# A graph layer's mix block: its second half moved into the edge batches

## The chip, the cores and the metric

The kernel runs on one NeuronCore of a Trainium2 chip. The metric is device time in microseconds (us) for one execution of the whole program. The program is one launch; every intermediate lies in on-chip memory or in scratch tensors in device memory.

## The reference, cut to what matters

A layer over 3125 nodes with 256 features each and 50000 edges sorted by target. `xn` is the layer norm of `x`. Three things are computed from it:

```python
xn  = layernorm(x)
# 1. graph attention: keys, queries, values by node type (6), edges of 3 types,
#    softmax over all the edges of a type, 8 heads
agg = segment_sum(w[..., None] * V[src] @ Wm[t], dst)
gnn = layernorm(agg + xn) * ln_g + ln_b
# 2. mix block (linear attention, 8 heads, then an MLP), here with its two halves
t   = linear_attention(elu(xn Wq) + 1, elu(xn Wk) + 1, xn Wv)
x1  = layernorm(t + xn) * ln1_g + ln1_b                     # first half
h   = gelu(x1 @ W1.T + b1)                                   # second half
mix = layernorm(h @ W2.T + b2 + x1) * ln2_g + ln2_b          # second half
x   = x + gnn + mix
# 3. a gated feed-forward part on layernorm(x): the top half of the rows by a score
x   = x + ffn(layernorm(x))
```

All sums are in float32. An output row needs the sum of its edges' messages, its mix row and its feed-forward row.

## The kernel before, in words

The nodes lie in NT = 25 tiles of 128 rows. The node tables (key and value rows, query rows) are made by node type in NS = 30 tiles, into which the rows are sorted. The edges lie in NB = 49 batches of two groups (NG = 98); a group gathers its key and value rows by four indirect DMAs of 256 KB on GpSimd's queue (POOL), into one of RING slots.

Every engine has its own instruction stream, written out by hand in the order in which it runs, and the streams meet at semaphores. There are four stages:

*Front*: layer norm of x, tables of the edges, the state of the linear attention.

*Tables and mix* (about 80 to 290 us): 30 steps, one per table tile. Step s works on table tile s and on mix tiles at several ages. TensorE (PE) runs in a step: mix_q, keys_values (L921), mix_t (L972) of the tile before, mix_turn (L996) of the one before that, queries (L932), mix_h (L985) of m-3, turn_in (L896) of the next table tile, by_type (L909), and mix_y (L1006, L1007) of m-4. turn_in turns the next tile's rows in bank ps[0], which queries uses too, so it waits until VectorE (DVE) has taken the queries out (g_qc). ScalarE (ACT) has in its step centre, the elu with an Exp (L776), affine (L784), a weights' copy, the gelu of m-3 (L794), turn_in's copy (L727) and q_out (L745). DVE has residual (L1299 to L1302), kv_out, elu, q_bias_in, attend, finish (L1308 to L1314) and shift. POOL has two pairs of reciprocal square roots (L657, L658), the product `gained` (L667), the load of the table rows two tiles ahead (L631) and the stores of the tables (L642, L648), all three indirect DMAs. SyncE (SP) loads rows of x (L531) and stores a finished mix row (L536); these rows are x + mix.

*Edges* (about 290 to 918 us): one pass of a software pipeline per batch b. The orders are:

- POOL: `rows_of(g)` (L1425), four gathers for group g; they wait until window_sums of g - RING + 1 have been made (semaphore yd).
- SP: `keys(b+1)` (L1393), which waits for ACT's distances, then `q_window(2b)` and `q_window(2b+1)` (L1384), which wait for PE's target_rows (qd).
- PE: target_rows(2b+1) (L1604), turn_sums (L1630), turn_maxima (L1648), window_sums(2b-3) (L1621), spread_maxima (L1655), turn_sums(2b-3), totals(b-1) (L1639), target_rows(2b+2), window_sums(2b-2).
- DVE: products(2b) (L1750, which reads what target_rows made), maxima, head_sums (L1757), maximum, products(2b+1), subtract, head_sums, weights, mark (L1769), messages(2b-2) and messages(2b-1) (L1809), then a piece of a search (L1853).
- ACT: keep_sums, distances (L1485, L1488), keep_rows(2b-3) (L1522, which takes window_sums out of PSUM), exponentials(b-1) (L1513), onehots, keep_sums, distances, keep_rows(2b-2), onehots.

RING is 7: six slots in the array `big`, one in `wmix`, where the mix block's weights lay before. Window_sums reads the messages, which stand where the gathered rows stood.

*Closing* (about 918 to 1167 us): sums over windows are scaled (L2062), turned into chunks of rows (L2315) and stored (L2138); then the rows of the graph attention are gathered, normalised and added to x + mix by DVE in pairs of tiles (`normalise_pair`; `stats_of` begins with L2415), turned (L2335) and put through the feed-forward matmuls (L2351, L2364). Three tiles are begun early, at steps STATS_AT = 13, 14, 15 of the scaling. SP loads feed-forward weights (L2112) in between and the rows of xn (L2127, xn_scratch).

## Time and profile before

| | |
|---|---|
| median of three runs | 1170.04 us |
| lowest and highest | 1167.43 and 1173.99 us |
| span of the profiled execution (its own time; no other is listed for it) | 1167.3 us |
| PE, DVE, POOL, ACT busy | 83%, 69%, 55%, 50% of the span |
| mean granted TensorE clock | 0.806 |

The busy shares are means over four stages that have different limits; the section on the rows has them by stage. "Clock" is the granted TensorE clock as a share of full speed. A wait that the profile puts down to "remote" is one whose releaser it doesn't find among the core's recorded instructions at that moment; "issue" is a wait for nothing that the profile shows. In the rows of a timeline, the bracket at the end is the idle time of the engine before the instruction and what ended it.

### The profile page before, as it was taken

How to read it: one execution, taken by the hardware profiler on the slowest of the kernel's cores; microseconds unless marked ns; L12 is line 12 of the kernel's file. 1: busy time of each engine (PE TensorE's matmuls, PEld its weight loads, DVE VectorE, ACT ScalarE, POOL GpSimd, SP SyncE). 2: the span in 40 equal slices, each digit the busy share in tenths (PEclk: the TensorE clock that was granted, in tenths of full speed). 3: DMA queues.
4: the chain of work that ended last, by engine and by line, in shares of the span. 5: the costliest groups of instructions: out<-in, count | busy, mean ns of one | idle time of the engine just before them, and what ended most of it. 6: DMA issues, size and time to landing. Idle time of an engine off the chain costs nothing.

```text
span 1167.3 us, 18084 instructions
## 1 busy us (share of the span) xinstructions
PE 967.1 (83%) x5053; PEld 677.5 (58%) x5053; DVE 803.3 (69%) x1708; ACT 587.4 (50%) x1534; POOL 640.5 (55%) x818
## 2 busy tenths in 40 slices
PE   5989999997157788777877878778778898999998
PEld 4767777775034444444444444444444687888886
DVE  7755888885256777777767677776767677887541
ACT  2657999983234554555545455554555322322220
POOL 4516788886725666666656666565664025664000
PEclk9999999999565766666667666666776799999999
DMA  9722544444736776766767767677674274210020
GB/s 294 220 71 104 159 145 145 146 146 174 234 114 182 208 212 210 205 204 203 214 202 214 210 198 211 201 211 208 201 211 146 69 226 152 79 46 19 1 86 25
DMA packets 112091, 189.89 MB, mean 163 GB/s; under 512 B 18187, under 2 KB 80734, under 8 KB 111990
## 3 DMA queue, kind: packets, MB, share of 16 engines
q0 software_dynamic: 38992, 129.87, 36.1%
q1 hardware_dynamic: 69718, 55.57, 15.7%
q10 hardware_dynamic: 3280, 3.28, 0.8%
q8 instruction: 43, 0.70, 0.2%
q14 instruction: 58, 0.48, 0.1%
HBM read 154.21 MB, written 34.44 MB: 162 GB/s over the span
## 4 chain that ended last, share of the span: by engine, by line
PE 55%; ACT 12%; issue 11%; another core or an unknown queue 10%; DVE 9%; DMA 1%; SPq 1%; POOL 0%; DVEq 0%; ACTq 0%; POOLq 0%
PE ps L2364 7%; PE ps L1621 7%; PE ps L2351 7%; PE ps L1604 6%; PE ps L921 4%; ACT edge L1500 4%; PE ps L2315 3%; PE ps L932 2%; PE ps L909 2%; PE ps L960 2%; ACT edge L1488 2%; PE ps L985 2%; ACT edge L1485 1%; PE ps L1639 1%
## 5 line engine op out<-in xcount | busy, mean ns | idle before, releaser
L1425 POOL DMA_INDIRECT big<-kv_scratch,src_i x336 | 317.8, 946 | 203.0 <-issue 89.8
L1604 PE MATMUL ps<-edge 64*128 64x256 f32 x784 | 177.6, 595 | 39.0 <-issue 38.8
L1750 DVE TENSOR_TENSOR big<-big,ps 128x1024 f32<-128x1024 f32 x84 | 101.6, 1210 | 121.3 <-PE ps L1604 61.9
L1621 PE MATMUL ps<-big,edge 128*64 128x256 f32 x672 | 149.4, 590 | 19.3 <-issue 10.3
L1604 PEld LDWEIGHTS ps<-edge 64*128 64x128 f32 x784 | 104.7, 289 | 89.5 <-issue 75.1
L1522 ACT ACTIVATE edge<-ps 128x256 f32<-128x256 f32 x98 | 37.6, 383 | 213.3 <-remote 146.0
L1621 PEld LDWEIGHTS ps<-big,edge 128*64 128x64 f32 x672 | 63.2, 199 | 78.6 <-issue 70.0
L1500 ACT ACTIVATE edge<-edge 128x64 f32<-128x64 f32 x392 | 102.9, 334 | 0.0
L1757 DVE TENSOR_REDUCE ps<-big 128x32 f32<-128x1024 f32 x84 | 102.3, 1218 | 0.1
L1809 DVE TENSOR_TENSOR big<-big,ps 128x1024 f32<-128x1024 f32 x84 | 98.9, 1209 | 0.0
L2351 PE MATMUL ps<-big 128*128 128x256 f32 (+2 forms) x416 | 88.7, 368 | 2.8 <-ACT big L2264 2.8
L2364 PE MATMUL ps<-big 128*128 128x256 f32 (+1 forms) x400 | 90.0, 380 | 0.0
L2277 ACT ACTIVATE big<-ps,fb 128x256 f32<-128x256 f32 (+2 forms) x104 | 39.4, 461 | 99.8 <-PE ps L2351 99.8
L1630 PE MATMUL ps<-ident,edge 128*128 128x128 f32 x196 | 53.6, 365 | 41.2 <-ACT edge L1522 32.7
L2351 PEld LDWEIGHTS ps<-big 128*128 128x128 f32 x416 | 74.3, 190 | 11.8 <-ACT big L2264 2.7
L2364 PEld LDWEIGHTS ps<-big 128*128 128x128 f32 (+1 forms) x400 | 73.6, 188 | 10.6 <-issue 0.3
L1425 POOL DMA_INDIRECT wmix<-kv_scratch,src_i x56 | 53.1, 948 | 30.8 <-issue 15.0
L1488 ACT ACTIVATE edge<-edge,ones 128x256 f32<-128x256 f32 x98 | 49.8, 508 | 29.4 <-remote 20.3
L1630 PEld LDWEIGHTS ps<-ident,edge 128*128 128x128 f32 x196 | 23.4, 168 | 68.7 <-ACT edge L1522 51.3
L921 PE MATMUL ps<-big,edge 128*128 x120 | 56.9, 596 | 0.5 <-ACT edge L727 0.3
L1485 ACT ACTIVATE edge<-edge,iota_n 128x256 f32<-128x256 bf16 x98 | 48.7, 497 | 13.9 <-DMA edge<-key_scratch 13.8
L1504 ACT ACTIVATE edge<-edge,ones 128x256 f32<-128x256 f32 x98 | 49.8, 508 | 8.9 <-issue 0.4
(354 smaller groups left out, 1919.0 us busy)
## 6 DMA issues: line engine op xcount, KB each, us to landing
edge<-q_scratch SPq DMA_DIRECT2D x196, 64.0 KB
edge<-key_scratch SPq DMA_DIRECT2D x98, 64.0 KB
big<-kv_scratch,src_i POOLq DMA_INDIRECT x336
agg_scratch<-big SPq DMA_DIRECT2D x16, 252.0 KB
xn_scratch<-big ACTq DMA_DIRECT2D x5, 640.0 KB, 5.4
mix_scratch<-big SPq DMA_DIRECT2D x25, 128.0 KB
big<-xn_scratch SPq DMA_DIRECT2D x25, 128.0 KB, 2.6
edge<-in_x SPq DMA_DIRECT2D x24, 128.0 KB
```

What stands on the lines that cost most here:

```text
L921: ins = pe.matmul(ps[1][:, :], xgT[:, t.k, ch * P:(ch + 1) * P], wall[:, ds(ty, 1), ch, 0:2 * D].rearrange("p a o -> p (a o)"), start=(ch ...
L1425: pool.indirect_dma_start(kv_slots[s][:, k, :], None, kv_d[0:N, :], bass.IndirectOffsetOnAxis(ap=src_i[:, e:e + 1], axis=0)).then_inc(got[ ...
L1488: act.activation(ohT[:, g % 2, :], dist, ACT.Relu, bias=ones[:, 0:1], scale=-1.0).then_inc(oh, 1)
L1500: ins = act.activation(gap[:, 2 * k + hg, :], iota_m, ACT.Abs, bias=neg_key[:, e:e + 1])
L1604: ins = pe.matmul(qr_ps[g % 2][:, (2 * hg + k) * D:(2 * hg + k + 1) * D], ohT[64 * hg:64 * hg + 64, g % 2, k * P:(k + 1) * P], qwin[64 * h ...
L1621: ins = pe.matmul(sums_of(g)[64 * hg:64 * hg + 64, :], oneh[:, s, k, hg * 64:hg * 64 + 64], kv_slots[s][:, 2 * hg + k, D:2 * D], start=(k ...
L1630: ins = pe.transpose(sums_of(g)[:, ch * P:(ch + 1) * P], rows_of_sums(g)[:, ch * P:(ch + 1) * P], ident[:, :])
L1750: dve.tensor_tensor(k_rows, k_rows, qr_ps[g % 2].rearrange("p (k d) -> p k d", d=D), ALU.mult).then_inc(pr, 1)
L1757: dve.tensor_reduce(scr[:, g // 2 % 2, (g % 2) * EG * H:(g % 2 + 1) * EG * H].rearrange("p (k h) -> p k h", h=H), kv_slots[g % RING][:, :, ...
L1809: dve.tensor_tensor(v, v, wgt[:, g // 2 % 2, (g % 2) * EG * H:(g % 2 + 1) * EG * H] .rearrange("p (k h d) -> p k h d", h=H, d=1).to_broadc ...
L2351: ins = pe.matmul(hslot[q % 2][:, j * GT * P:j * GT * P + w], fw1[:, ch, f * P:(f + 1) * P], cols[:, ch, at:at + w], start=(ch == 0), stop ...
L2364: ins = pe.matmul(ps[4 + t % 2][0:m, 0:D], fh[:, p % 2, f, at:at + m], fw2[:, f, :], start=(f == 0), stop=(f == FJ - 1))
```

## The change

Only the first half of the mix block stays in the table stage. It ends with `affine`, whose result x1T (turned, 128 x 256) SP stores to scratch, 128 KB for each of 25 tiles. mix_h, the gelu, mix_y, residual, finish, `gained` and the second pair of roots leave the stage; DVE keeps one sum there (`with_x`: x + ln2_b), which is what SP stores as the mix row. turn_in gets a bank of its own (ps[7]), goes ahead of mix_t on PE, and its copy and the weights' go ahead of affine on ACT; POOL loads table rows three tiles ahead.

The second half of mix tile m goes into the edge batches, from batch MIX_FROM[m] = 7 + 3m//2 on (7, 8, 10, 11, 13, ... 43). SP loads the tile's x1T in its loop one later, mix_h is the last thing that PE does in its loop MIX_FROM; in the next loop follow the gelu on ACT (behind distances, ahead of keep_rows and exponentials), mix_y on PE (ahead of totals; two of its four matmuls add x1 by the identity), and on DVE mix_row (ahead of the messages), mix_stats (between them), mix_var and mix_gain (behind them). SP stores the centred and gained row x2 in its loop MIX_FROM + 5. The array wmix keeps the MLP's weights and the buffers of x1 and x2, two each, so RING is 6.

In the closing POOL makes all 25 reciprocal roots in one go, SP loads x2 back tile by tile, and DVE adds it to the stored mix row, scaled (`prepare_row`), before the row is used. The semaphores are given out in another order, and the branch for several passes, which is not run with these inputs, has some more waits. The core of the diff (names of engine and stage put in at the hunks):

```diff
@@ -30,8 +30,8 @@
-RING = 7
-RING_BIG = RING - 1
+RING = 6
+RING_BIG = RING
...
+MIX_FROM = [7 + 3 * m // 2 for m in range(NT)]
+X1_LAG, X2_LAG = 1, 5
...
+X2_AT = (14, 15)
...
+    x1_d = scratch("mix_x1_scratch", (NT, P, D))
+    x2_d = scratch("mix_x2_scratch", (NP, D))
...
+        x1e = wmix[:, 0:2 * D].rearrange("p (k d) -> p k d", d=D)
+        x2e = wmix[:, 3 * C * D:3 * C * D + 2 * D].rearrange("p (k d) -> p k d", d=D)
...
@@ SyncE, table stage @@
+                    seen(sp, m_x1, t)
+                    sp.dma_start(x1_d[t.t, :, :], x1T[:, t.t % 3, :]).then_inc(m_x1st[t.k], 16)
...
@@ GpSimd, table stage @@
+                load(Tile(1, 0, NS))
                 for s in range(NS + 1):
                     t, m = Tile(s // 2, s % 2, NS), Tile(s // 2, s % 2, NT)
-                    roots(m.at(-5), m_c, m_r2, 1)
-                    gained(m.at(-2))
-                    load(t.at(2))
                     store_kv(t.at(0))
-                    roots(m.at(-1), m_tx, m_r1, 0)
+                    load(t.at(3))
+                    roots(m.at(-1), m_tx, m_r1)
                     store_q(t.at(-1))
...
@@ ScalarE, table stage @@
-                    act.activation(xgT[:, t.k, :], ps[0][:, 0:D], ACT.Copy).then_inc(g_Tc, 1)
+                    act.activation(xgT[:, t.k, :], ps[7][:, 0:D], ACT.Copy).then_inc(g_Tc, 1)
...
-                    seen(act, m_y, t.at(-3))
+                    seen(act, m_x1st, t.at(-3), 16)
...
-                def gelu(t):
-                    if t is None:
-                        return
-                    seen(act, m_h, t)
-                    seen(act, m_y, t.at(-2))
-                    for j in range(C):
-                        ins = act.activation(hT[:, t.k, j * P:(j + 1) * P], ps[7][:, j * P:(j + 1) * P], ACT.Gelu,
-                                             bias=b1c[:, j:j + 1])
-                    ins.then_inc(m_g, 1)
...
+                    weights(t.at(1))
+                    turn_in(t.at(1))
                     affine(m.at(-2))
-                    weights(t.at(1))
-                    gelu(m.at(-3))
-                    turn_in(t.at(1))
@@ TensorE, table stage @@
-                    seen(pe, g_qc, t.at(-1))
+                    seen(pe, g_Tc, t.at(-1))
                     seen(pe, g_in, t, 16)
                     for ch in range(C):
-                        ins = pe.transpose(ps[0][:, ch * P:(ch + 1) * P], xg[:, t.k, ch * P:(ch + 1) * P], ident[:, :])
+                        ins = pe.transpose(ps[7][:, ch * P:(ch + 1) * P], xg[:, t.k, ch * P:(ch + 1) * P], ident[:, :])
...
+                    seen(pe, g_qc, t.at(-1))
...
+                pe.wait_ge(s_bad, 2)
...
-                def mix_h(t):
-                    if t is None:
-                        return
-                    if t.t == 0:
-                        pe.wait_ge(s_vec, 16 * N_VEC)
-                    seen(pe, m_x1, t)
-                    seen(pe, m_g, t.at(-1))
-                    for o in range(C):
-                        for ch in range(C):
-                            ins = pe.matmul(ps[7][:, o * P:(o + 1) * P], w1T[:, ch, o * P:(o + 1) * P],
-                                            x1T[:, t.t % 3, ch * P:(ch + 1) * P], start=(ch == 0), stop=(ch == C - 1))
-                    ins.then_inc(m_h, 1)
...
-                def mix_y(t):
-                    if t is None:
-                        return
-                    seen(pe, m_g, t)
-                    seen(pe, m_x1, t.at(2))
-                    seen(pe, m_c, t.at(-1))
-                    y_ps = ps[6][:, 0:D]
-                    pe.matmul(y_ps, hT[:, t.k, 0:P], w2T[:, 0, :], start=True, stop=False)
-                    ins = pe.matmul(y_ps, hT[:, t.k, P:2 * P], w2T[:, 1, :], start=False, stop=True)
-                    ins.then_inc(m_y, 1)
...
+                    turn_in(t.at(1))
                     mix_t(m.at(-1))
                     mix_turn(m.at(-2))
                     queries(t.at(0))
-                    mix_h(m.at(-3))
-                    turn_in(t.at(1))
                     by_type(t.at(-1))
-                    mix_y(m.at(-4))
@@ VectorE, table stage @@
-                def residual(t):
+                def with_x(t):
                     if t is None:
                         return
-                    seen(dve, m_y, t)
...
+                    dve.tensor_tensor(mo[:, t.k, :], xr[:, t.k, :], vecs["L0_mix_ln2_b"][:, :], ALU.add).then_inc(m_out, 1)
 
                 for s in range(NS + 1):
                     t, m = Tile(s // 2, s % 2, NS), Tile(s // 2, s % 2, NT)
-                    residual(m.at(-5))
                     ty = kv_out(t.at(0))
                     elu(m.at(0))
+                    attend(m.at(-1))
                     q_bias_in(t.at(0), ty)
-                    attend(m.at(-1))
-                    finish(m.at(-5))
+                    with_x(m.at(-2))
@@ SyncE, edge stage @@
+                def load_x1(m):
+                    at_least(sp, yp, m - 1)
+                    sp.dma_start(x1e[:, m % 2, :], x1_d[m, :, :]).then_inc(x1in[m % 2], 16)
+
+                def store_x2(m):
+                    sp.wait_ge(yg, m + 1)
+                    sp.dma_start(x2_d[m * P:(m + 1) * P, :], x2e[:, m % 2, :]).then_inc(x2st[m % 2], 16)
...
+                    for m in mix_tiles(b, X1_LAG):
+                        load_x1(m)
+                    for m in mix_tiles(b, X2_LAG):
+                        store_x2(m)
@@ ScalarE, edge stage @@
+                def mix_gelu(m):
+                    act.wait_ge(hp, m + 1)
+                    at_least(act, yp, m)
+                    for j in range(C):
+                        ins = act.activation(hTe[:, j * P:(j + 1) * P], h_ps_e[:, j * P:(j + 1) * P], ACT.Gelu,
+                                             bias=b1c[:, j:j + 1])
+                    ins.then_inc(hk, 1)
...
+                    for m in mix_tiles(b, 1):
+                        mix_gelu(m)
                     keep_rows(2 * b - 3)
                     exponentials(b - 1)
@@ TensorE, edge stage @@
+                def mix_h(m):
+                    pe.wait_ge(x1in[m % 2], 16 * (m // 2 + 1))
+                    at_least(pe, yr, m)
+                    for o in range(C):
+                        for ch in range(C):
+                            ins = pe.matmul(h_ps_e[:, o * P:(o + 1) * P], w1T[:, ch, o * P:(o + 1) * P],
+                                            x1e[:, m % 2, ch * P:(ch + 1) * P], start=(ch == 0), stop=(ch == C - 1))
+                    ins.then_inc(hp, 1)
+
+                def mix_y(m):
+                    pe.wait_ge(hk, m + 1)
+                    for ch in range(C):
+                        pe.matmul(y_ps_e, hTe[:, ch * P:(ch + 1) * P], w2T[:, ch, :], start=(ch == 0), stop=False)
+                    for ch in range(C):
+                        ins = pe.matmul(y_ps_e[:, ch * P:(ch + 1) * P], x1e[:, m % 2, ch * P:(ch + 1) * P], ident[:, :],
+                                        start=False, stop=(ch == C - 1))
+                    ins.then_inc(yp, 1)
...
                     turn_sums(2 * b - 3)
+                    for m in mix_tiles(b, 1):
+                        mix_y(m)
                     totals(b - 1)
                     target_rows(2 * b + 2)
                     window_sums(2 * b - 2)
+                    for m in mix_tiles(b, 0):
+                        mix_h(m)
@@ VectorE, edge stage @@
+                def mix_row(m):
+                    dve.wait_ge(yp, m + 1)
+                    at_least(dve, x2st[m % 2], 16 * (m // 2))
+                    dve.tensor_tensor(x2e[:, m % 2, :], y_ps_e, vecs["L0_mix_b2"][:, :], ALU.add).then_inc(yr, 1)
+
+                def mix_stats(m):
+                    dve.wait_ge(yr, m + 1)
+                    dve.bn_stats(x2s, x2e[:, m % 2, :]).then_inc(ya, 1)
+
+                def mix_var(m):
+                    dve.wait_ge(ya, m + 1)
+                    dve.bn_aggr(x2v[:, m, :], x2s).then_inc(yv, 1)
+
+                def mix_gain(m):
+                    dve.wait_ge(yv, m + 1)
+                    dve.scalar_tensor_tensor(x2e[:, m % 2, :], x2e[:, m % 2, :], x2v[:, m, 0:1], vecs["L0_mix_ln2_g"][:, :],
+                                             ALU.subtract, ALU.mult).then_inc(yg, 1)
...
                     mark(b)
+                    for m in mix_tiles(b, 1):
+                        mix_row(m)
                     messages(2 * b - 2)
+                    for m in mix_tiles(b, 1):
+                        mix_stats(m)
                     messages(2 * b - 1)
+                    for m in mix_tiles(b, 1):
+                        mix_var(m)
+                        mix_gain(m)
                     if b >= SEARCH_AT:
                         search(c, b - SEARCH_AT, 1)
@@ SyncE, closing @@
+                def load_x2(t):
+                    if t >= NT:
+                        return
+                    at_least(sp, rp, t - 1)
+                    sp.dma_start(x2e[:, t % 2, :], x2_d[t * P:(t + 1) * P, :]).then_inc(x2in[t % 2], 16)
...
+                load_x2(0)
+                load_x2(1)
...
+                    if k in X2_AT:
+                        load_x2(2 + X2_AT.index(k))
...
-                for t in range(GR, NT):
-                    load_xn(t)
+                for t in range(4, NT):
+                    if t + 4 >= GR and t + 4 < NT:
+                        load_xn(t + 4)
+                    load_x2(t)
@@ GpSimd, closing @@
+                pool.wait_ge(yv, NT)
+                pool.tensor_scalar(x2v[:, :, 1], x2v[:, :, 1], EPS_LN, None, ALU.add).then_inc(s_x2r, 1)
+                pool.wait_ge(s_x2r, 1)
+                pool.tensor_tensor(x2r, x2v[:, :, 1], nhalf[:, :], ALU.pow).then_inc(s_x2r, 1)
@@ VectorE, closing @@
+                def prepare_row(i):
+                    dve.wait_ge(s_x2r, 2)
+                    dve.wait_ge(mix_in[i // 2 % 3], 16 * (i // 6 + 1))
+                    dve.wait_ge(x2in[i % 2], 16 * (i // 2 + 1))
+                    dve.scalar_tensor_tensor(rows[:, i, :], x2e[:, i % 2, :], x2r[:, i:i + 1], rows[:, i, :], ALU.mult, ALU.add
+                                             ).then_inc(rp, 1)
...
+                    dve.wait_ge(rp, i + 1)
...
+                    prepare_row(a)
                     stats_of(a)
                     stats_of(b)
+                    prepare_row(b)
...
                     if k in STATS_AT:
+                        prepare_row(k - STATS_AT[0])
                         stats_of(k - STATS_AT[0])
                         gained(k - STATS_AT[0])
-                dve.wait_ge(mix_in, 16 * len(MIX_PARTS))
```

## Rows read from the trace of the kernel before

**Rows 1.** Windows: us; PE, PEld, DVE, ACT, POOL busy (instructions); clock; DMA share; GB/s.

```profile
85.00:250.00 165.00, 163.21 (x1079) 129.06 (x1078) 127.27 (x364) 147.89 (x287) 127.43 (x175) 1.00 0.41 141
...
350.00:880.00 530.00, 417.71 (x1884) 233.02 (x1882) 383.40 (x559) 279.44 (x829) 329.70 (x349) 0.66 0.69 205
1000.00:1100.00 100.00, 100.00 (x488) 87.69 (x487) 76.33 (x259) 28.27 (x76) 49.65 (x89) 1.00 0.12 35
```

**Rows 2.** The chain that ended last, L921 in the table stage: start, us.

```profile
85.38 1.81 PE ps L921 x4
...
281.82 1.72 PE ps L921 x4
```

**Rows 3.** Timeline of one table step: start us, us, engine, line, operation, out<-in.

```profile
185.72 1.28 ACT L776 ACT_TABLE_LOAD   x1
...
187.02 0.42 ACT L776 ACTIVATE big<-big 128x256 f32<-128x256 f32 x1
...
187.79 1.06 PE L985 MATMUL ps<-big,wmix 128*128 128x128 f32 x8
...
188.69 0.43 PE L896 MATMUL ps<-ident,edge 128*128 128x128 f32 x2
...
189.90 0.70 PE L1006 MATMUL ps<-wmix,big 128*128 128x256 f32 x2
189.96 0.63 ACT L794 ACTIVATE big<-ps,b1c 128x128 f32<-128x128 f32 x2
...
190.87 1.05 PE L960 MATMUL ps<-big,wmix 128*128 128x128 f32 x8
```

**Rows 4.** Timeline of one edge batch.

```profile
696.01 0.94 POOL L1425 DMA_INDIRECT big<-kv_scratch,src_i  x1 [2.40 <-remote]
...
701.48 0.80 PE L1639 MATMUL ps<-ones,edge 128*96 128x1 f32 x4 [0.22 <-issue]
...
702.21 2.08 PE L1604 MATMUL ps<-edge 64*128 64x256 f32 x8
...
702.62 2.34 DVE L1809 TENSOR_TENSOR big<-big,ps 128x1024 f32<-128x1024 f32 x2
...
704.21 1.97 PE L1621 MATMUL ps<-big,edge 128*64 128x256 f32 x8
...
704.77 0.94 POOL L1425 DMA_INDIRECT big<-kv_scratch,src_i  x1 [0.31 <-issue]
...
707.71 0.38 ACT L1522 ACTIVATE edge<-ps 128x256 f32<-128x256 f32 x1 [3.47 <-remote]
707.72 1.22 DVE L1750 TENSOR_TENSOR big<-big,ps 128x1024 f32<-128x1024 f32 x1 [2.42 <-remote]
707.95 0.94 POOL L1425 DMA_INDIRECT big<-kv_scratch,src_i  x1 [2.24 <-remote]
```

**Rows 5.** Waits from 350 to 880 us: total us, times, longest.

```profile
ACT edge L1522 <- remote: 139.5, 37, 4.5
```

**Rows 6.** Windows before and after the batch's restart.

```profile
705.70:707.60 1.90, 1.90 (x12) 1.19 (x8) 0.00 (x0) 0.00 (x0) 0.01 (x1) 0.50 0.81 263
708.40:709.40 1.00, 0.19 (x2) 0.00 (x0) 1.00 (x3) 0.91 (x4) 0.70 (x2) 1.00 0.14 34
```

**Rows 7.** Timeline around 380 us, with short bursts of gathers.

```profile
377.59 2.08 PE L1604 MATMUL ps<-edge 64*128 64x256 f32 x8
...
380.26 1.21 DVE L1750 TENSOR_TENSOR big<-big,ps 128x1024 f32<-128x1024 f32 x1
```

**Rows 8.** Timeline at the end of the first fill of the ring.

```profile
330.31 1.22 DVE L1750 TENSOR_TENSOR big<-big,ps 128x1024 f32<-128x1024 f32 x1 [9.88 <-remote]
```

**Rows 9.** Timeline of the closing, around step 15 of the scaling.

```profile
969.58 0.41 SPq L2112 DMA_DIRECT2D big<-in_L_ffn_w  x1
970.10 0.42 DVE L2415 TENSOR_TENSOR big<-big 128x256 f32<-128x256 f32 x1
```

**Rows 10.** The page, DMA issues, rows of xn: KB each, us to landing.

```profile
big<-xn_scratch SPq DMA_DIRECT2D x25, 128.0 KB, 2.6
```

96 lines of the change are left out of this document (48 added, 48 removed).

## The prediction

> **What bounds the kernel now.** I read the span by stages first. Between 85 and 250 us, where the tables and the mix layer are made, the granted clock is full (1.00, so 2.4 GHz) and PE is busy 163.21 of 165.00 us: PE sets the pace, with ACT (147.89) close behind [rows 1]. The step's length is in the chain of waits: the projection matmuls of L921 start at 85.38 and at 281.82, with 28 steps between them, so 7.02 us a step [rows 2]. In the edge batches (350 to 880 us) no engine is full: PE 417.71 of 530, DVE 383.40, POOL 329.70, ACT 279.44, DMA 0.69 [rows 1]. Here the order of waits decides, and I read one batch event by event.
>
> POOL issues eight gathers between 696.01 and 704.77 (1.25 us apart) and the next burst starts at 707.95, so a batch lasts 11.94 us. What ends it is odd. PE's records of target_rows end at 702.21 + 2.08 = 704.29 and those of window_sums at 704.21 + 1.97 = 706.18; yet DVE (waiting for target_rows), ACT and POOL (waiting for window_sums) all start together at 707.71 to 707.95, after idle times of 2.42, 3.47 and 2.24 us that the profile puts down to no matmul ("remote") [rows 4]. That moment is the one at which the DMA engines run empty: their share is 0.81 up to 707.6 and 0.14 from 708.4 on [rows 6]. I call it the hold: from the second half of a burst, whoever waits for PE starts when the burst has drained, some 11.7 us after it began. Where POOL's bursts were short, it isn't there: target_rows ended at 379.67 and DVE went on at 380.26 [rows 7]. It is no accident of one batch: ACT's wait of that kind stands 37 times in 530 us, so in 37 of about 44 batches (530 / 11.94), 0.84 of them [rows 5].
>
> After 1000 us PE is full again, DVE has 24 us in 100 to spare [rows 1].
>
> **The change, part by part.**
>
> *Table stage.* PE loses mix_h (187.79 to 188.69, when the next operation starts: 0.90) and mix_y (189.90 to 190.87: 0.97) [rows 3], so 1.87 of 7.02 us. ACT loses the gelu (0.63) and both table loads, 1.28 each [rows 3]: without Gelu, one table is left. That takes it from 147.89 / 165 x 7.02 = 6.3 to about 3.1 us. POOL loses a product and a pair of roots out of 127.43 / 165 x 7.02 = 5.4 us; DVE drops the seven operations of residual and finish and gains with_x, so its 127.27 falls too [rows 1]. The bank ps[7] for the turned rows lets turn_in go ahead of mix_t and of queries' copy; POOL's order (a table's store, then the load of three tiles ahead, roots, the query store) has one operation fewer than now. On SP a 128 KB store of the turned rows goes in behind the mix row; the affine step waits for a store three tiles old, the next tables' load is issued ahead of it, so neither is late. New pace: at least 7.02 - 1.87 = 5.15 (PE), at most POOL's 5.4 with its waits, some 5.8. I take 5.5, as POOL's chain of indirect transfers won't follow PE wholly: 28 x 1.52 = **-42 us** (between -34 and -52).
>
> *Start of the edge stage.* With six ring slots instead of seven the first fill is 24 gathers, not 28. DVE's second products wait 9.88 us there in the same hold [rows 8]. Four gathers less, 1.25 us each [rows 4], end it 5 us earlier: **-5** (0 to -6). In the steady batches one slot less moves each gather one release later; the gathers of a group are issued a burst before DVE asks for them, and it asks some 3 us into the next: nothing, while a burst still lands by then. If that cover is gone, DVE waits for rows instead.
>
> *Edge batches with a mix tile,* 25 of 49, two in a row and then one without. ACT: a Gelu load 1.28, the gelu 0.63 and an Exp load 1.28 before exponentials: 3.19 us [rows 3], behind distances and ahead of keep_rows. ACT has the room in total (279.44 of 530, so 6.3 a batch, and 3.19 more is 9.5 of 11.94), but the second turn_sums and totals wait for it. PE: mix_y comes right before totals (701.48, so 5.5 us into the burst) and then ends some 8 to 9 us into it: 0.97 at full clock; twice that at the lower level of 1.2 GHz, where the stage's mean of 0.66 [rows 1] says it often is. mix_h at the end of the batch goes in the time in which all wait for the hold.
>
> DVE: mix_row waits for mix_y, in front of both messages. The records give mix_y no reason to be seen before 707.7: its place is between totals and target_rows, and what PE ended from there on was held. Then behind it queue: mix_row 0.42 (as a 128x256 row costs at 970.10 [rows 9]), the first of the messages 1.17 (half of 2.34), for which window_sums waits (1.97), for which POOL's next gathers wait (0.24, from 707.71 to 707.95) [rows 4]. Burst start + 11.70 + 0.42 + 1.17 + 1.97 + 0.24 = 15.50 in place of 11.94: +3.56. Statistics, the second messages, variance and gain follow in DVE's idle time. In the 0.16 of batches without the hold the tail of PE is only pushed by ACT's 3.19: 706.18 + 3.19 + 0.24 = 709.61 for 707.95, +1.66. The mean is 0.84 x 3.56 + 0.16 x 1.66 = 3.26, and 25 of them **+81 us**. Bounds of a tile: 0 (all of it in the 2.24 us in which POOL idles, if mix_y is seen at once and early) and 4.4 (a hold, and PE at half clock in the tail).
>
> Two transfers of 128 KB per tile join the drain. SP issues the load (X1_LAG) and the store (X2_LAG) in one place, behind the q_windows of a loop, which in time is about 4 us into a burst. At 263 GB/s [rows 6] the 256 KB are 0.97 us, if nothing is free; nothing, if engines are. SP's keys and q_windows queue behind the waits of both, whose signals (yp, yg) are batches old. I take 0.2 a tile, since the DMA share of the stage is 0.69: **+5** (0 to +24).
>
> *Closing.* 25 prepare_row of 0.42 to 0.48 go into DVE's spare time next to a full PE [rows 1]. One isn't covered: in step k = 15 the third prepare_row, in front of the statistics at 970.10 [rows 9], needs rows whose load SP issues behind the weights at 969.58 + 0.41; with 2.6 us from issue to landing [rows 10] it is there at 972.6, 2.5 us late, and the last scale is queued behind it. Later tiles' rows come in one by one with the loads of x's rows behind the totals: another 1 to 2 for the first pair. POOL's 25 roots in one instruction have the whole second half to end in. **+4.5** (0.5 to 8).
>
> *Semaphores renumbered, mix_in split into three, waits in the branch of several passes* (not run: one pass): nothing.
>
> **Sum,** against the profiled execution's span of 1167.3 us; its own time isn't listed apart, the three runs have a median of 1170.04, 2.7 above, which I don't add. 1167.3 - 42 - 5 + 81 + 5 + 4.5 = 1210.8, say **1211 us**.
>
> The page "ScalarE: Activation LUTs" of the Trainium skill (What ACT_TABLE_LOAD costs) states a drain of some 1.38 us on top of the load's 1.28. In this trace the load at 185.72 ends at 187.00 and the next activation starts at 187.02 [rows 3], so no such drain is seen, and the measurement decides. By the rule a mix batch would cost two drains, 2.76 us, more on ACT: nothing under the hold, 25 x 2.76 = 69 us where mix_y is seen at once.
>
> **The rivals.**
>
> *A, the forecast:* mix_row waits out the hold, 1211 us. For it: three engines released at one moment in 0.84 of the batches. Against it: the batches with short bursts.
>
> *B, no hold on mix_y* (DVE's longer wait breaks the bursts into fours, as around 380, and waits end at once): only ACT's push remains, 25 x 1.66 = 42: 1167.3 - 42 - 5 + 42 + 4.5 = 1167, no change.
>
> *C, the other side: all of it is hidden.* DVE, PE and ACT each have over 2 us a batch idle; if mix_row is released before the first message would have started anyway and PE's tail stays under the drain, the batch remains 11.94 us: 1167.3 - 42 - 5 + 4.5 = 1125. It decides from the point at which window_sums still ends by 707.7, that is, with PE's tail pushed by under 1.5 us. ACT's 3.19 speaks against it.
>
> *D, transfers bind:* the added 256 KB lengthen each drain by the full 0.97, and a store that mix_row waits for lands with it: 25 x 0.97 = 24 in place of 5, so 1230.
>
> *E, the table switch drains:* in B's case with the drains of the page above, worked out as a wait of ACT in each of the 25 batches: 1167 + 69 = 1236. The row at 187.02 speaks against it.
>
> That the change doesn't do what it says: the table stage keeps its pace because POOL's indirect transfers take PE's place at 7 us. POOL's 5.4 us a step speak against it; A would then be 1253. I fold it into the upper end.
>
> **How the numbers follow.** A 0.54, B 0.18, C 0.16, D 0.08, E and the last 0.04 together. About 0.5% (6 us) is what a measurement of this kernel tells from no change. B lies within it half of the time and on each side a quarter: 0.09 same, 0.05 faster, 0.04 slower. Faster: 0.16 + 0.05 and a 0.03 of A with small terms = 0.24; same 0.09 + 0.01 = 0.10; slower the rest, 0.66. The range reaches from within C (1134) to within D and E (1236); A's own is 1190 to 1232.
>
> **What would show it.** L921 every 5.5 us, no table load in that stage, POOL not fuller than PE. In a mix batch: a long idle time of DVE in front of mix_row that ends when the DMA share drops, POOL's bursts 15.5 us apart there and 12 in the third batch; the step is wrong if mix_row starts within 1 us of mix_y's end, or if all bursts stay 12 us apart (C). Two table loads of 1.28 a mix batch, with the next activation right behind (else E). DVE idle for 2 to 3 us at the third prepare_row. The forecast falls altogether if the edge stage isn't longer.

## The result and the profile after

The changed kernel took 1163.01 us, the median of 20 runs (1150.72 to 1183.73), beside 1169.47 us for the kernel before, 20 runs (1163.89 to 1183.02). The ratio is 0.9923, with a 95% interval of 0.9901 to 0.9946: 0.8% faster, where 1211 us and slower were forecast. Ratios here leave out executions more than 1.5% above the fastest of their kernel (7 of the 20 after, 2 of the 20 before); the two medians alone give 0.9945. The profiled execution has a span of 1160.2 us, 7.1 less than before.

I cut both spans at the same instructions, DVE's first products of an edge batch (L1750 before, L1765 after). After, the timeline of DVE has these rows (start us, us, engine, line, operation); they open the first, the second, the 8th and the 46th batch:

```profile
252.25 1.22 DVE L1765 TENSOR_TENSOR big<-big,ps 128x1024 f32<-128x1024 f32 x1 [0.58 <-issue]
...
274.70 1.22 DVE L1765 TENSOR_TENSOR big<-big,ps 128x1024 f32<-128x1024 f32 x1 [4.19 <-remote]
...
346.93 1.22 DVE L1765 TENSOR_TENSOR big<-big,ps 128x1024 f32<-128x1024 f32 x1 [1.93 <-remote]
...
845.65 1.22 DVE L1765 TENSOR_TENSOR big<-big,ps 128x1024 f32<-128x1024 f32 x1
```

Before, the same cuts lie at 301.86, at 330.31 [rows 8], and for the 8th and the 46th batch here:

```profile
405.86 1.22 DVE L1750 TENSOR_TENSOR big<-big,ps 128x1024 f32<-128x1024 f32 x1 [1.60 <-PE ps L1604]
...
865.22 1.22 DVE L1750 TENSOR_TENSOR wmix<-wmix,ps 128x1024 f32<-128x1024 f32 x1 [2.72 <-remote]
```

| stretch (us) | before | after | difference | forecast |
|---|---|---|---|---|
| start to the first products | 301.9 | 252.3 | -49.6 | -42 |
| first to second batch | 28.5 | 22.5 | -6.0 | -5 |
| second to 8th batch | 75.5 | 72.2 | -3.3 | 0 |
| 8th to 46th batch, all 25 mix tiles | 459.4 | 498.7 | +39.4 | +86 |
| to the last products (901.33; 883.57) | 36.1 | 37.9 | +1.8 | 0 |
| closing | 266.0 | 276.6 | +10.6 | +4.5 |
| sum | 1167.3 | 1160.2 | -7.1 | +43.5 |

So 59 us were won and 52 given back, where 47 and 90.5 were forecast. I call the fourth row **the stage**. Two cautions go with it. It comes from one profiled execution, and executions of one kernel differ by several us, so only differences above some 8 us of a stage are read below. And the kernel before, run beside each experiment, has medians from 1170.0 to 1176.6 us, so times of different experiments are compared by their ratios to it.

**Table stage.** In the chain of waits the projection matmuls, now L913, open and close 28 steps like this:

```profile
84.91 1.94 PE ps L913 x4
...
232.18 1.92 PE ps L913 x4
```

That is 147.3 us, 5.26 a step, beside 7.02 [rows 2]. Both are means over unequal steps: in the middle of the stage a step takes 5.44 us now (204.65 to 210.09) and took 7.24 before (191.92 to 199.16), and the last ones are shorter.

**Three stretches like those of rows 1**, now (us; PE, PEld, DVE, ACT, POOL busy; clock; DMA share; GB/s):

```profile
85.00:225.00 140.00, 139.11 (x908) 103.26 (x909) 93.12 (x276) 94.98 (x227) 101.24 (x128) 1.00 0.61 214
350.00:880.00 530.00, 404.25 (x2156) 266.71 (x2152) 394.29 (x624) 339.83 (x871) 310.28 (x328) 0.77 0.71 204
1000.00:1093.00 93.00, 91.50 (x446) 79.68 (x445) 76.65 (x257) 24.66 (x66) 44.40 (x81) 1.00 0.18 53
```

In the edge batches PE issues more (2156 for 1884 instructions) and is busy less; its granted clock went from 0.66 to 0.77.

**Who waits for whom in the edge batches** changed too. Waits of after, 350 to 880 us (engine, line, waited for: total us, times, longest):

```profile
POOL big L1401 <- PE ps L1611: 117.1, 55, 5.9
...
ACT edge L1500 <- remote: 31.5, 13, 4.7
...
POOL big L1401 <- remote: 22.4, 14, 2.4
...
DVE wmix L1910 <- PE ps L1670: 8.3, 9, 1.0
...
DVE wmix L1910 <- remote: 7.8, 2, 4.1
...
DVE wmix L1910 <- issue: 5.2, 6, 1.0
...
DVE wmix L1910 <- DMA mix_x_scratch<-wmix: 1.6, 1, 1.6
```

and of before:

```profile
POOL big L1425 <- remote: 75.8, 32, 2.7
...
POOL big L1425 <- PE ps L1621: 18.6, 8, 4.5
```

ACT's unexplained wait fell from 37 times [rows 5] to 13. POOL now waits 55 times for window_sums by name. A wait that bears PE's name did not always end with PE's records, though: of the 54 such waits of POOL that the timeline lists one by one, 29 end within 0.3 us of the end of window_sums and 25 end 0.5 to 3.0 us after it. Mix_row (L1910) had a long unexplained wait just twice in 25 tiles, and in 22 of them it started within 0.5 us of mix_y's end. One mix batch in the timeline of after shows how:

```profile
518.45 0.95 POOL L1401 DMA_INDIRECT big<-kv_scratch,src_i  x1 [1.42 <-PE ps L1611]
...
522.22 1.08 PE L1611 MATMUL ps<-big,edge 128*64 128x256 f32 x8 [0.45 <-issue]
...
523.09 1.28 ACT L1514 ACT_TABLE_LOAD   x1
524.39 0.63 ACT L1514 ACTIVATE edge<-ps,b1c 128x128 f32<-128x128 f32 x2
524.65 0.94 POOL L1401 DMA_INDIRECT big<-kv_scratch,src_i  x1 [1.50 <-PE ps L1611]
524.90 0.38 ACT L1500 ACTIVATE edge<-ps 128x256 f32<-128x256 f32 x1
525.31 1.28 ACT L1491 ACT_TABLE_LOAD   x1
...
525.82 1.91 PE L1668 MATMUL ps<-wmix,edge 128*128 128x256 f32 x4
...
526.60 0.36 ACT L1491 ACTIVATE edge<-edge 128x192 f32<-128x192 f32 x1
...
527.53 1.06 PE L1670 MATMUL ps<-ident,wmix 128*128 128x128 f32 x4
528.63 0.42 DVE L1910 TENSOR_TENSOR wmix<-ps,v_L_mix_b 128x256 f32<-128x256 f32 x1 [0.99 <-issue]
...
529.00 2.08 PE L1594 MATMUL ps<-edge 64*128 64x256 f32 x8
...
531.01 1.97 PE L1611 MATMUL ps<-big,edge 128*64 128x256 f32 x8
...
533.27 0.95 POOL L1401 DMA_INDIRECT big<-kv_scratch,src_i  x1 [3.91 <-PE ps L1611]
```

mix_y ends at 527.53 + 1.06 = 528.59 and mix_row starts 0.04 us later. POOL's eight gathers come as two fours, with waits of 1.50 and 3.91 us behind them. The second wait ends 0.29 us after window_sums (531.01 + 1.97 = 532.98), the first 1.35 us after it (522.22 + 1.08 = 523.30; POOL goes on at 524.65). From burst to burst the batch lasts 533.27 - 518.45 = 14.82 us. Over the stage, cut at DVE's first products, the 25 batches with a mix_y last 14.39 us on average (15.61 with the next tile's mix_h in them, 12 times; 13.26 without, 13 times), and the other 13 batches last 10.69, though each of them has a mix_h at its end. Before, these groups of batches had means of 12.06 to 12.12. The price of a tile is therefore +2.30 us in its own batch on average, and a third of it comes back in the batches between.

**Closing.** After, around the fifth prepare_row (L2495):

```profile
973.20 0.34 SPq L2173 DMA_DIRECT2D big<-xn_scratch  x1
973.60 0.42 SPq L2160 DMA_DIRECT2D wmix<-mix_x_scratch  x1
...
975.96 0.48 DVE L2495 SCALAR_TENSOR_TENSOR edge<-wmix,v_L_mix_ln_b,edge 128x256 f32<-128x256 f32 x1 [9.01 <-DMA wmix<-mix_x_scratch]
...
980.87 0.44 PE L2394 MATMUL ps<-ident,big 128*128 128x128 f32 x2 [3.26 <-DVE big L2519]
```

DVE waits 9.01 us for a row whose load SP issues at 973.60, and then PE waits 3.26 for DVE.

### The profile page after: what moved, and what is told of

Read it like the earlier page. It is cut to its first block, busy times and chain, and to the rows that moved or that the text cites. A ratio compares the mean times of both kernels' runs of the same rounds, so it can differ in the third digit from the quotient of the medians.

```text
span 1160.2 us, 18271 instructions
## 1 busy us (share of the span) xinstructions
PE 940.1 (81%) x5153; PEld 687.8 (59%) x5153; DVE 791.8 (68%) x1682; ACT 599.2 (52%) x1540; POOL 599.9 (52%) x745
## 4 chain that ended last, share of the span: by engine, by line
PE 52%; DVE 14%; issue 12%; ACT 9%; POOL 5%; another core or an unknown queue 5%; DMA 2%; SPq 1%; DVEq 0%; ACTq 0%; POOLq 0%
PE ps L1611 7%; PE ps L1594 6%; PE ps L2423 5%; PE ps L913 4%; PE ps L2410 4%; DVE big L1824 3%; PE ps L1620 3%; PE ps L2374 3%; PE ps L1668 2%; PE ps L954 2%; PE ps L925 2%; PE ps L901 2%; ACT L1514 2%; PE ps L1661 2%
## 5 line engine op out<-in xcount | busy, mean ns | idle before, releaser
L1401 POOL DMA_INDIRECT big<-kv_scratch,src_i x392 | 372.2, 950 | 266.1 <-PE ps L1611 136.2
L1594 PE MATMUL ps<-edge 64*128 64x256 f32 x784 | 148.8, 509 | 33.7 <-issue 21.4
L1611 PE MATMUL ps<-big,edge 128*64 128x256 f32 x784 | 142.1, 496 | 40.3 <-issue 20.8
L1765 DVE TENSOR_TENSOR big<-big,ps 128x1024 f32<-128x1024 f32 x98 | 118.5, 1209 | 52.7 <-remote 31.4
L1594 PEld LDWEIGHTS ps<-edge 64*128 64x128 f32 x784 | 88.9, 244 | 61.8 <-issue 49.0
L1772 DVE TENSOR_REDUCE ps<-big 128x32 f32<-128x1024 f32 x98 | 119.4, 1218 | 0.1
L1824 DVE TENSOR_TENSOR big<-big,ps 128x1024 f32<-128x1024 f32 x98 | 116.5, 1207 | 0.0
L2410 PE MATMUL ps<-big 128*128 128x256 f32 (+2 forms) x416 | 92.8, 381 | 2.8 <-ACT big L2323 2.8
L2423 PEld LDWEIGHTS ps<-big 128*128 128x128 f32 (+1 forms) x400 | 73.6, 188 | 10.6 <-issue 0.3
L1466 ACT ACTIVATE edge<-edge,ones 128x256 f32<-128x256 f32 x98 | 49.8, 508 | 23.8 <-issue 10.4
L913 PE MATMUL ps<-big,edge 128*128 x120 | 57.2, 598 | 0.0
L1506 ACT ACTIVATE big<-ps 128x252 f32<-128x252 f32 x98 | 35.9, 368 | 39.3 <-PE ps L1620 23.5
L2374 PE MATMUL ps<-bd_m,big 128*126 128x128 f32 (+1 forms) x396 | 48.4, 284 | 9.2 <-DVE big L2102 7.4
```

The source lines that it names most:

```text
L913: ins = pe.matmul(ps[1][:, :], xgT[:, t.k, ch * P:(ch + 1) * P], wall[:, ds(ty, 1), ch, 0:2 * D].rearrange("p a o -> p (a o)"), start=(ch ...
L1401: pool.indirect_dma_start(kv_slots[s][:, k, :], None, kv_d[0:N, :], bass.IndirectOffsetOnAxis(ap=src_i[:, e:e + 1], axis=0)).then_inc(got[ ...
L1594: ins = pe.matmul(qr_ps[g % 2][:, (2 * hg + k) * D:(2 * hg + k + 1) * D], ohT[64 * hg:64 * hg + 64, g % 2, k * P:(k + 1) * P], qwin[64 * h ...
L1611: ins = pe.matmul(sums_of(g)[64 * hg:64 * hg + 64, :], oneh[:, s, k, hg * 64:hg * 64 + 64], kv_slots[s][:, 2 * hg + k, D:2 * D], start=(k ...
L1765: dve.tensor_tensor(k_rows, k_rows, qr_ps[g % 2].rearrange("p (k d) -> p k d", d=D), ALU.mult).then_inc(pr, 1)
L1772: dve.tensor_reduce(scr[:, g // 2 % 2, (g % 2) * EG * H:(g % 2 + 1) * EG * H].rearrange("p (k h) -> p k h", h=H), kv_slots[g % RING][:, :, ...
```

## The experiments

In each, "expected" is the text recorded before the run. Edits are against the changed kernel, unless "of before" is said.

**Is it ACT's table loads?** e1 puts Relu in gelu's place, with which no table is loaded in the edge batches.

```diff
-ins = act.activation(hTe[:, j * P:(j + 1) * P], h_ps_e[...], ACT.Gelu,
+ins = act.activation(hTe[:, j * P:(j + 1) * P], h_ps_e[...], ACT.Relu,
```

> The changed kernel (1163 us) with a Relu in the place of the Gelu in the edge batches, so that no table is loaded there: the gelu itself is left out of the computation. Theory S (serial chain): a mix batch is longer because ACT's table load and gelu come before keep_rows, and turn_sums, mix_y, mix_row and the messages follow one after the other. The 1.28 us of the Gelu load is on that chain, the Exp load runs beside mix_y: 25 x 1.28 = 32 us less, 1131 us (1125 to 1143). Theory T (throughput of VectorE): the 1.5 us of mix work per tile on DVE make the batch longer, wherever it stands: no change, 1163. Theory H (mix_row waits out the drain of the gathers): no change either, 1163.

Measured: 1172.34 us, with 1176.33 for before beside it (no interval), the stage 498.7 us, as with Gelu. No gain is seen, but little is settled: the four runs go from 1152.32 to 1174.22, and the profiled one took 1172.06. So ACT's push, visible in the batch above, isn't shown to be what the tile costs, nor ruled out.

**Is it mix_row's place on DVE?** e2 moves mix_row and the statistics behind both messages.

```diff
-for m in mix_tiles(b, 1): mix_row(m)
 messages(2 * b - 2)
-for m in mix_tiles(b, 1): mix_stats(m)
 messages(2 * b - 1)
+for m in mix_tiles(b, 1): mix_row(m); mix_stats(m)
```

> The changed kernel with mix_row, mix_stats, mix_var and mix_gain all behind both messages; the same work on every engine. Theory S: the messages and with them window_sums no longer wait for mix_y (some 1 us of idle time) and for mix_row (0.42): 25 x 1 to 1.4, so 1128 to 1140 us. Theory T: the same DVE work, no change, 1163. Theory H: the wait moves behind the messages, where the drain is over: as much as the hold costs, 25 x 1.57 = 39 less, 1124.

Measured: ratio 0.9841 (0.9788 to 0.9895), so better than the change by 0.8% if the two ratios are set side by side, from four runs and with a profiled stage of 498.2. If the place costs something, this profiled execution doesn't locate it.

**What does all mix work in the edge batches cost?** e3 leaves it out.

```diff
-return [m for m in range(NT) if MIX_FROM[m] + lag == b]
+return []
```

> The changed kernel with all of the mix work in the edge batches left out (loads of x1, mix_h, gelu, mix_y, mix_row to mix_gain, stores of x2): the second half of the mix block is not computed, and the closing adds other rows. It prices the rest of the change by itself. All theories: the batches are 12.05 us long again, with POOL's bursts of eight and the hold, so 1163 - 39 = 1124 us (1118 to 1132). If the edge batches without mix work stay under 12 us, the six ring slots or the new start are what made the batches between the mix tiles shorter.

Measured: 0.9665 (0.962 to 0.9711), the stage 470.1. The mix work costs (0.9923 - 0.9665) x 1170 = 30 us by the times and 28.6 by the stages, 1.2 us a tile. So of the 39.4 us that the stage grew by, some 11 are there without any mix work. That is from single executions: e9 and r6 below, which have six slots too, put it at 2 and 7. The forecast had left the steady batches' sixth slot at nothing. Without the mix work, bursts are of eight again (38 of 39), and the hold is back; waits of e3, 350 to 815 us:

```profile
ACT edge L1500 <- remote: 139.6, 35, 6.1
POOL big L1401 <- remote: 89.8, 35, 2.9
```

**Is it the transfers?** e8 moves 16 of 128 partitions; e9 makes both transfers and leaves out the work between them (a constant tile is stored).

```diff
-sp.dma_start(x1e[:, m % 2, :], x1_d[m, :, :])
+sp.dma_start(x1e[0:16, m % 2, :], x1_d[m, 0:16, :])
```

> The changed kernel with all of the mix work of the edge batches on PE, ACT and DVE, but its two transfers cut from 128 to 16 partitions (16 KB each in place of 128 KB); most of x1 is not loaded and most of x2 not stored. The moves of the table loads (e1) and of mix_row (e2) changed nothing in the edge stage. Theory D (bytes): the edge stage moved 203 to 205 GB/s before, in the changed kernel and in both of these runs, so it is bound by what the transfers carry, and the 25 x 256 KB = 6.55 MB of a mix tile's load and store cost 6.55 / 0.204 = 32 us. The stage from the 8th to the 46th batch falls from 498 to about 470 us and the time to that of the kernel without mix work, 1140 us (1132 to 1146). Theory T (work on DVE and PE, wherever it stands): 498 us, 1163.

> The kernel without mix work in the edge batches, with SP's 25 loads of x1 and 25 stores of 128 KB put back at their places, with no compute behind them (the second half of the mix block is left out). Theory D: the transfers alone bring the stage from 470 to about 498 us, and the time to 1163 (1156 to 1170). Theory T: it stays 470 us and 1140 (1134 to 1146).

Measured: e8 0.9925 (0.9877 to 0.9973), the same as the change; e9 0.9693 (0.9611 to 0.9775), which lies within e3's interval, with a stage of 461.8. The 256 KB a tile cost nothing that can be measured.

**Is the hold the drain of the gathers' bytes?** h1, of before, gathers half of each row (the value half is a constant).

```diff
-pool.indirect_dma_start(kv_slots[s][:, k, :], None, kv_d[0:N, :],
+pool.indirect_dma_start(kv_slots[s][:, k, 0:D], None,
+                        kv_d[0:N, :].rearrange("n (a d) -> (n a) d", a=2),
```

> The kernel before with gathers of half the bytes: each row brings 256 numbers in place of 512 (128 KB a gather, the value half of a row is left out and stands at a constant), the same 8 gathers a batch on POOL. If the hold is the drain of the DMA queue, it ends with POOL's last gather, and a batch takes POOL's 8 x 1.25 = 10 us and little more, 10.2 to 10.8 in place of 12.07: 49 x 1.3 to 1.9 = 64 to 93 us less than the kernel before. If it hangs on POOL's issuing alone (PE's results seen 2 us after the last one), the batch stays 12 us, and only the first fill gets shorter: 0 to 10 us less.

Measured: 1.0011 (0.9971 to 1.0051). The stage of h1 as a window (columns as above):

```profile
405.93:865.57 459.64, 368.14 (x1634) 205.68 (x1634) 335.73 (x495) 243.14 (x722) 287.61 (x304) 0.65 0.43 120
```

and of before:

```profile
405.86:865.22 459.36, 364.92 (x1634) 203.22 (x1634) 335.36 (x496) 243.12 (x722) 287.70 (x304) 0.66 0.70 207
```

120 GB/s instead of 207, and the stage is the same within 0.3 us. The hold stands as before; waits of h1, 350 to 880 us:

```profile
ACT edge L1525 <- remote: 144.2, 38, 4.9
```

Only the first fill became short, 5.5 us for 28.5, and that is gone by the 8th batch: the start is 8 us later here (310.0; the constant half has to be written), and from the second to the 8th batch it takes 90.4 us for 75.5. So the moment at which three engines are released together [rows 4] isn't set by bytes. The trace of before could have said so: from 707.4 to 707.8, while ACT and DVE are released (707.71), the queue of the gathers is still at work, as the row below shows (packets, MB, share of the 16 engines); it falls to 16% only after 708.0. The windows of [rows 6] leave out the time between.

```profile
q0 software_dynamic: 29, 0.11, 69.6%
```

What came is the other branch of the expectation, the hold that "hangs on POOL's issuing alone". The end of a burst of h1:

```profile
705.73 0.95 POOL L1426 DMA_INDIRECT big<-kv_scratch,src_i  x1 [0.30 <-issue]
...
708.89 0.38 ACT L1525 ACTIVATE edge<-ps 128x256 f32<-128x256 f32 x1 [4.46 <-remote]
```

ACT is released 2.21 us after the end of POOL's last gather, and 2.00 before (704.77 + 0.94, then 707.71 [rows 4]). Over 350 to 880 us POOL's wait behind a burst of eight lies between 2.05 and 2.71 us in all 41 cases of before and between 2.05 and 2.86 in all 41 of h1, while the same waits of before end anything from 1.4 to 3.9 us after the records of window_sums. Behind bursts of four, in the changed kernel, it is 1.20 at least, and 1.5 in the middle of 54 cases. The release keeps time with POOL's bursts; that POOL causes it is not shown.

**Is it the length of the bursts?** s1, of before, puts three small memsets (0.74 us) in front of each four gathers.

```diff
+for j in range(3):
+    at_least(pool, hz, 3 * g + j)
+    pool.memset(gapt[:, :], 0.0).then_inc(hz, 1)
```

> The kernel before with three small memsets on POOL ahead of each group of four gathers (some 0.6 to 0.9 us), so that its bursts of eight are broken into fours; no other change. h1 showed that the hold doesn't hang on the bytes. Theory P (the hold comes with POOL issuing eight gathers on end): the waits that the profile calls remote nearly vanish, target_rows is seen within 1 us of its end, and the batch becomes 11 to 12.4 us, so between -50 us and +15 of before; POOL's own 2 x (5.0 + 0.8) = 11.6 is the floor. Rival (any 8 gathers per batch, however spaced, hold PE's results until the last is out): the waits stay, and the batch gets longer by the memsets, 12.07 + 1.6: +75 us.

Measured: 0.9959 (0.9928 to 0.999), 77 bursts of four, and the hold stays. One batch of s1:

```profile
504.14 0.95 POOL L1430 DMA_INDIRECT big<-kv_scratch,src_i  x1 [0.30 <-issue]
...
505.98 0.95 POOL L1430 DMA_INDIRECT wmix<-kv_scratch,src_i  x1 [0.15 <-issue]
...
507.86 1.97 PE L1626 MATMUL ps<-big,edge 128*64 128x256 f32 x8
...
509.76 1.28 PE L1609 MATMUL ps<-edge 64*128 64x256 f32 x8
...
510.70 0.74 POOL L1426 MEMSET gapt<- 128x128 f32 x3
...
512.34 0.38 ACT L1527 ACTIVATE edge<-ps 128x256 f32<-128x256 f32 x1 [4.17 <-remote]
512.35 1.22 DVE L1755 TENSOR_TENSOR big<-big,ps 128x1024 f32<-128x1024 f32 x1 [3.40 <-PE ps L1609]
```

window_sums ended at 509.83 and ACT, which waits for it, starts 2.5 us later, though POOL's last burst is a four. Over 350 to 880 us ACT's wait of this kind stands 39 times with 159.5 us. So bursts of four with a gap of 0.9 us in the middle of a batch (504.14 + 0.95 = 505.09 to 505.98) don't remove the hold. The gaps of the changed kernel are longer, 1.20 us at least; whether such gaps would remove it was not tried.

**Does the seventh ring slot matter?** r6, of before, has `RING = 6`.

> The kernel before with six ring slots in place of seven and nothing else changed. By the prediction's step: the first fill ends 5 us earlier, the steady batches are as they were: 0 to 6 us less than before. By its rival, from the kernel without mix work (12.37 us a batch in place of 12.07): the seventh slot was worth 0.3 us a batch, 38 x 0.3 = 11 and more over all batches, so 5 to 10 us slower than before.

Measured: 0.9996 (0.9956 to 1.0035). From the first to the second batch it takes 22.5 us for 28.5, as after the change, and the time is no shorter: the 8th batch starts at 405.6, as before, so the gain is gone by then. Its stage is 466.5, but in an execution 7 us above its own median, so that figure isn't read as a price.

**Is it the amount of work on DVE or on PE?** e10 does DVE's mix operations on 8 columns, e11 the mix matmuls on 8 columns.

```diff
-dve.tensor_tensor(x2e[:, m % 2, :], y_ps_e, vecs["L0_mix_b2"][:, :], ALU.add)
+dve.tensor_tensor(x2e[:, m % 2, 0:8], y_ps_e[:, 0:8], vecs["L0_mix_b2"][:, 0:8], ALU.add)
...
-pe.matmul(y_ps_e, hTe[...], w2T[:, ch, :], start=(ch == 0), stop=False)
+pe.matmul(y_ps_e[:, 0:(8 if m else D)], hTe[...], w2T[:, ch, 0:(8 if m else D)], ...)
```

> The changed kernel with DVE's four operations of a mix tile on 8 columns in place of 256 (the rest of x2 is left out), PE's and ACT's work as it is. DVE's share of a tile falls from 1.5 us to some 0.5. Theory T-DVE (VectorE's added work sets the longer batches): 25 x 1.0 = 25 us less, 1138 us, the price of the mix work. Theory T-PE (TensorE's added work at the low clock sets them): no change, 1163 (1155 to 1170).

> The changed kernel with mix_h and mix_y of all tiles but the first on 8 columns in place of 128 or 256 (the rest of h and y is left out), ACT's and DVE's work as it is. In a mix batch of the changed kernel's profile mix_h takes 2.08 us, and mix_y 1.91 and 1.06, on a PE whose clock is half in the second part of a batch. Theory T-PE: these 4.6 us fall to under 1, and with them the 25 to 29 us that the mix work costs: 1138 (1132 to 1146). Theory T-DVE: no change, 1163.

Measured: e10 0.995 (0.9919 to 0.9981), stage 499.3: DVE's work on the columns is not the price. e11 1.0084 (1.005 to 1.0117), stage 515.4: with **less** work for PE the kernel is 1.6% slower than the change. Its window over 350 to 880 us, beside the changed kernel's above:

```profile
350.00:880.00 530.00, 421.19 (x2080) 278.22 (x2080) 382.94 (x610) 331.87 (x847) 296.05 (x314) 0.67 0.68 197
```

The granted clock is 0.67 for 0.77, and PE is busy longer (421.19 for 404.25) with fewer columns. e12 has e11's and e1's edits together.

> The changed kernel with e1 and e11 together: a Relu for the Gelu (no table load in the edge batches) and the matmuls of all tiles but the first on 8 columns; most of h and y and the gelu are left out, DVE's work of a tile stays. Theory O (two costs that overlap: ACT's loads and gelu ahead of keep_rows, 3.2 us, and PE's matmuls, 4.6 us at the low clock; with either one left the batch is as long, so taking one away brought nothing): with both gone the stage from the 8th to the 46th batch is 470 to 480 us, as without mix work, and the time 1140 to 1150. Theory K (the clock alone: whatever takes work from PE makes the stage longer): as e11, 515 us and 1184.

Measured: 0.997 (0.9947 to 0.9993), stage 506.2, clock 0.65. Without the table loads the light version is 1.1% faster than e11; so there ACT's table loads do cost, at a clock that is no higher.

**Does added PE work pay itself back?** f1, of before, adds two dummy matmuls of 128x256 to each batch ahead of turn_maxima; f2 two more ahead of totals; f3 puts f1's into the changed kernel.

```diff
+def fill(b, n): ...
+    for _ in range(n):
+        pe.matmul(ps[1][:, 256:512], ident[:, :], vecs["L0_gnn_ln_g"][:, :], start=True, stop=True)
...
+fill(b - 2, 2)
```

> The kernel before with two more matmuls of 128x128 by 256 columns in each edge batch, whose result nobody reads, where PE waits for the maxima (ahead of turn_maxima): 0.85 us at the full clock, 1.7 at the half. The computation is complete. Theory C (clock): PE runs at the low level in 67% of the edge stage because it idles in the first half of a batch, and the results that are seen late are those of a PE that is behind; the filler lifts the share of the full clock (0.33 before, 0.54 in the changed kernel, 0.34 in e11 with light matmuls), the waits called remote shrink, and a batch gets 0.5 to 1.5 us shorter: 25 to 70 us less than before. Rival W (only the amount of work counts): PE isn't waited for in that place for longer than 0.95 us, so the batch gets 0 to 0.8 us longer: 0 to +40 us.

> As f1, with two more such matmuls ahead of totals in each batch. Theory C: the clock's share rises further; faster than before, and more so than f1 if f1 leaves the share under 0.6. Rival W: another 0.85 to 1.7 us of PE work on the way to target_rows: 40 to 80 us slower than before.

> The changed kernel with f1's two matmuls per batch, ahead of turn_maxima. Theory C: as in f1, the share of the full clock rises above 0.54, and the stage from the 8th to the 46th batch falls from 498 us to 480 or less; 1163 - 18 or more. Rival W: 0 to 0.8 us a batch longer, 0 to +40 us.

Measured: f1 1.0331 (1.0274 to 1.0387), stage 501.6; f2 1.0225 (1.0166 to 1.0283), stage 481.6; f3 0.9989 (0.9949 to 1.003), stage 490.0, at a clock of 0.85, but in an execution of 1161.4 us, 9 below its own median. By the ratios f3 is 0.7% slower than the change. The window of f1:

```profile
350.00:880.00 530.00, 396.69 (x1892) 236.49 (x1890) 356.85 (x522) 259.62 (x762) 303.17 (x322) 0.72 0.66 189
```

and of f2:

```profile
350.00:880.00 530.00, 407.08 (x2142) 263.60 (x2141) 371.69 (x539) 268.21 (x792) 316.25 (x335) 0.81 0.68 198
```

Twice the filler costs less than once (1188.6 to 1198.4 us for 1205.8 to 1210.7), with the clock at 0.81 for 0.72. In f1 the hold moved to another wait, DVE's for its maxima (350 to 880 us):

```profile
DVE mall L1794 <- remote: 91.0, 21, 5.0
```

Over its stage f1's filler keeps PE busy for 45.6 us, and the stage is 42.3 us longer; f2's takes 99.2 us, and the stage is 22.2 longer. Neither the filler's length nor the clock nor the hold explains both sizes.

**Is it that all pieces fall in one place?** e6 spreads them over two batches.

```diff
 # ACT: gelu behind the second distances, then an Exp of one column
 # PE:  mix_y(m) for mix_tiles(b, 2), behind the first turn_sums
 # DVE: mix_row for mix_tiles(b, 2), behind the second products
```

> The changed kernel with the same mix work at other places, none of it in a chain within one batch: the gelu behind the second distances on ACT, with a small Exp behind it that brings the other table back while ACT waits; mix_y one batch later, behind the first turn_sums; mix_row behind the second products, and the statistics and the gain behind both messages. Theory T-PE or T-DVE (amount of work): 1155 to 1163 us, as for e1 and e2, which moved one part each. Theory S in a wider form (each of e1 and e2 left another part of the chain standing, and any part is enough): the batches go back to some 12.4 us, 1163 - 25 = 1138.

Measured: 0.9973 (0.9951 to 0.9994), stage 500.7. Nothing is won.

**The closing.** e4 prepares 12 rows in steps 4 to 15 of the scaling; c1 six rows in steps 10 to 15, each load two steps ahead.

```diff
-X2_AT = (14, 15)
+PREP_AT, PREP_N = 10, 6      # e4: 4, 12
...
+if PREP_AT <= k < PREP_AT + PREP_N:
+    load_x2(k - PREP_AT + 2)         # SP, step k
...
+    prepare_row(k - PREP_AT)         # DVE, step k
```

> The changed kernel with twelve of the prepare_row brought forward, one in each of the steps 4 to 15 of the closing's scaling, and the loads of x2 ahead of them by two steps; the later rows nine tiles ahead of their use. In the profile of the changed kernel DVE stands 3.9 us before the third and 9.0 us before the fifth prepare_row, and the closing is 10.6 us longer than before. Theory C1 (the loads of x2 come too late): these two waits go, 1163 - 8 to 10 = 1153 to 1155 us. Theory C2 (the closing is longer because DVE has 25 operations more): no change, 1163, or 1 us more, since a step of the scaling has under 0.34 us to spare on DVE.

> The changed kernel with only six prepare_row brought forward (steps 10 to 15 of the scaling, in place of e4's twelve from step 4), loads two steps ahead. e4 gave 8 us back behind the scaling (191.8 in place of 199.4 us from the tails' gather to the end), but its twelve operations lengthened the scaling by 7. Theory C1: the 3.9 us and the 9.0 us waits still go, and six operations, three of which were there already, cost 3 us at most: 1163 - 4 to 8 = 1155 to 1159, a ratio to before of 0.985 to 0.989. Theory C2 (nothing to be had): 0.992.

Measured: e4 0.9874 (0.9811 to 0.9937), c1 0.9866 (0.9822 to 0.991), each some 0.5% below the change with intervals that meet its own. From POOL's second gather of tails to the end it is 191.8 and 191.5 us, beside 1160.2 - 960.75 = 199.4 in the change: 8 us. In e4 the scaling itself grows by 7 us, in c1 it doesn't.

**A better version.** c2 is c1 with e2's order of DVE, the whole computation in it.

> c1 together with e2 (mix_row and what follows it behind both messages), all of the computation kept. e2 was at 0.984 of before, with an interval of 0.979 to 0.990, against 0.992 of the changed kernel. If the two add up: 0.978 to 0.985 of before. If e2's was noise: as c1.

Measured: 1145.44 us (1143.13 to 1150.52, 6 runs) beside 1170.76: 0.9801 (0.9754 to 0.9847), below the interval of the change. Its stage is 484.3 at a clock of 0.80; why that is shorter than e2's 498.2, with the same order of DVE, is not shown. Its closing part is 1141.4 - 949.77 = 191.6. The longest wait for a row is 4.7 us now (waits of c2, DVE, 930 to 1000 us):

```profile
DVE edge L2493 <- DMA wmix<-mix_x_scratch: 9.7, 5, 4.7
```

## Why the prediction was wrong

The measured 1163 us lies inside the forecast's range of 1134 to 1236 because that range was drawn across the rivals; the way the time would go, and the reason, were wrong.

**Table stage (-42; measured -49.6): right, mis-sized.** The step became PE's, as worked out; 5.26 us a step lies at the floor of 5.15, not at the 5.5 chosen because "POOL's chain of indirect transfers won't follow PE wholly". POOL followed: in the middle of the stage a step lost 1.80 us, where PE lost 1.87 by the forecast.

**Start (-5; -6.0): right** in size. In r6, where only the ring is changed, it isn't a net gain: by the 8th batch it is gone.

**Mix batches (+81; +39.4 with the transfers' +5): the step that failed.** It is "mix_row waits for mix_y, in front of both messages. The records give mix_y no reason to be seen before 707.7 ... what PE ended from there on was held", priced at +3.56 in 0.84 of the batches. The forecast's own test, mix_row within 1 us of mix_y's end, came out against it: 0.04 us in the batch shown, under 0.5 us in 22 of 25 tiles, and long unexplained waits at L1910 in 2. Two assumptions were under that step. One was that a hold seen in a fixed order of work stays when the order changes; it faded (ACT's from 37 to 13), while e3 and e9, without the mix work, had it back or ran in bursts of eight. The other was that it is the drain of the burst; h1 has 120 GB/s in place of 207 and the same hold, so a loose coincidence with the DMA share [rows 6] was read as a cause. The wait that took its place is POOL's and ACT's for window_sums, and in 29 of 54 cases of POOL's it ends with PE's work. The sum also took mix_y at 0.97 us of full clock, the two matmuls of before; the changed one has four, and took 2.77 us in the batch shown (525.82 to 528.59). The batches without a mix_y, which the forecast left at 11.94 us, fell to 10.69 and gave 13 x 1.4 = 18 us back, out of the 25 x 2.30 = 57.5 us that the tiles cost in their own batches.

**Rival B came near the time (1167) by luck, its reason is not borne out.** Bursts did fall into fours, and about half of POOL's waits did end at once. But its price was ACT's push, 25 x 1.66 = 42 us, and the mix work's whole price was 30; e1 takes the loads away, and its profiled stage is as long. Its cause for the fading was the short bursts; s1 has fours, with short gaps, and the hold together.

**What a tile's 1.2 us are stays open.** Transfers (e8, e9) and DVE's columns (e10) are excluded as its cause, spreading the pieces (e6) brought nothing, table loads alone (e1) are unsettled, and fewer columns on PE made it worse (e11). It may be that PE's added work is partly paid for by the clock that it raises, 0.66 to 0.77. For it: e11 beside the change, and f2 beside f1, have the higher clock with more PE work, and less time with it. Against it: f1 has a higher clock than before (0.72 for 0.66) and is 3.3% slower, and e12 has a lower one than e11 (0.65 for 0.67) and is faster. All of them change the order of the waits as well, so that isn't settled. What the hold is stays open, too. The releases keep time with POOL's bursts, with half of the bytes as with all, but no run changed POOL's issuing enough to show a cause.

**Transfers (+5; nothing): mis-sized**, inside its range. **Tables' drain: not seen**, as forecast: the load at 523.09 ends at 524.37 and gelu starts at 524.39; the load at 525.31 ends at 526.59 and the next activation starts at 526.60. The drain that the Trainium skill states (ScalarE: Activation LUTs, What ACT_TABLE_LOAD costs) doesn't show here either, nor ahead of the second load, which starts 0.03 us after the activation at 524.90 ends.

**Closing (+4.5; +10.6): the mis-sized term.** The third row was near (a wait of 3.94 us in front of it, at 952.97, for the 2.5 forecast). "Another 1 to 2 for the first pair" was the miss: the fifth row's load stands on SP behind the stores of the totals and costs DVE 9.01 us. c1 shows what of it can be had back, 8 us.

## To carry to other kernels

A wait without a named cause that ends together with some counter isn't shown to be caused by it; look at the moment itself in fine windows, and change the counter's quantity alone (half the bytes here), before a forecast rests on it. Where the order of waits sets the pace and no engine is full, price added work as a range that includes what the neighbours give back, and look at the batches between. For loads that an added operation needs, find the place in the issuing queue and everything ahead of it: that term was certain, and doubled.

## Of the hardware

Two things I had not expected. Waits for PE that end 1.5 to 4.4 us after the record of the matmuls' end stayed with half of the gathers' bytes (144.2 us in 38 waits, for 139.5 in 37) and with gaps of 0.9 us between the gathers (159.5 in 39). And in a stage with waits the granted clock rose with added matmuls and fell with lighter ones, and the time went neither with the clock nor with the amount of work: 0.67 for 0.77, and 1.6% slower than the change, with light matmuls; 0.72 and 0.81 for 0.66 with two and four dummies, the four costing 2.3% where the two cost 3.3%. The Trainium skill (TensorE: Matmul & The Clock Gate, Part 1) says of this clock that "the default state is throttled, and activity releases the throttle"; the direction of the clock agrees with these rows.
